# Four edge hops gather with no bounds check, and targets without out-edges read a row of zeros

## The reference, cut to what matters

```
src = randint(0, 100000, (50000,));  dst = randint(0, 100000, (50000,))
A = 0.9 * segment_softmax(scores, head_ids)          # one weight per edge and head, 4 heads
Z = broadcast(x[:, None, :], (N, 4, 64))
for _ in range(5):
    Z = segment_sum(A[:, :, None] * Z[tail_ids], head_ids) + 0.1 * x[:, None, :]
out = Z.reshape(N, 256) @ W_o
```

## Time and profile before

| | us |
|---|---|
| median of 3 runs | 12004.88 (11990.27 to 12047.62) |
| the profiled execution | 12010.07 |
| its span, first to last instruction | 12007.8 |
| hop 1, first gather to hop 2's first gather | 543.5 |
| GpSimd busy | 7991.8 (67%) |
| VectorE busy | 6262.3 (52%) |

### The profile page before, as it was taken

The page is one execution under the profiler, slowest core; times in us unless marked ns, Lnnn a source line. Parts: engine busy times, 40 slices in busy tenths (PEclk is TensorE's granted clock), DMA queues, the critical chain, the costliest instruction groups (busy, mean ns, idle before and its releaser), DMA issues. The chain is left out here.

```text
span 12007.8 us, 102357 instructions
## 1 busy us (share of the span) xinstructions
PE 5179.3 (43%) x22423; PEld 3584.6 (30%) x22423; DVE 6262.3 (52%) x12751; ACT 2459.6 (20%) x4317; POOL 7991.8 (67%) x7869
## 2 busy tenths in 40 slices
PE   1719994000000244445656678843335422222245
PEld 1403331000000144444444556622224322222234
DVE  8931115767878644465545669943336533321127
ACT  0102221022222211122323333310003200000035
POOL 1767774776767677753767666657767677777730
PEclk9959997555555555566767777755556555555578
DMA  2412222544545311167655556622229833311148
GB/s 107 165 20 58 57 58 72 167 136 151 165 149 166 104 40 42 41 215 211 168 155 167 178 185 191 194 75 59 59 54 312 246 65 65 65 47 46 46 152 251
DMA packets 1247797, 1471.21 MB, mean 123 GB/s; under 512 B 843713, under 2 KB 948738, under 8 KB 1244410
## 3 DMA queue, kind: packets, MB, share of 16 engines
q1 hardware_dynamic: 951992, 1127.40, 29.7%
q0 software_dynamic: 277328, 269.94, 10.7%
q10 hardware_dynamic: 18290, 72.03, 1.5%
HBM read 830.95 MB, written 772.36 MB: 134 GB/s over the span
## 5 line engine op out<-in xcount | busy, mean ns | idle before, releaser
L2541 POOL DMA_INDIRECT r_got<-state,comb_src x1176 | 1218.2, 1036 | 449.3 <-issue 350.1
L328 POOL DMA_INDIRECT payload_or_bias_rows<-payload,place x784 | 875.5, 1117 | 669.6 <-issue 260.4
L1330 POOL DMA_INDIRECT hop_got<-edges_b,next_col x784 | 790.7, 1009 | 271.8 <-issue 238.0
L1330 POOL DMA_INDIRECT hop_got<-edges_a,next_col x784 | 783.4, 999 | 265.5 <-issue 238.2
L1579 PE MATMUL hop_ps_into<-hop_out,span_s 128*128 128x256 f32 (+1 forms) x10 | 5.6, 660 | 2046.4 <-DVE hop_out L1471 2045.1
L1519 ACT COPY hop_got<-hop_zeros 128x1792 f32<-128x1792 f32 x224 | 377.4, 1685 | 1514.9 <-DVE hop_ps_msg L1422 1102.8
L1579 PEld LDWEIGHTS hop_ps_into<-hop_out,span_s 128*128 128x128 f32 x10 | 2.5, 311 | 2048.9 <-DVE hop_out L1471 2047.3
L1471 DVE SCALAR_TENSOR_TENSOR hop_out<-hop_out,hop_runs_now,hop_ps_msg 128x256 f32<-128x256 f32 x1176 | 565.5, 481 | 51.0
L1342 POOL DMA_INDIRECT sum<-hop_out,put_s x392 | 432.2, 1103 | 119.5 <-issue 119.5
L2678 DVE TENSOR_REDUCE r_stat<-r_sq 128x14 f32<-128x896 f32 x196 | 211.9, 1081 | 571.1 <-ACT r_sq L2848 570.8
L2549 POOL DMA_INDIRECT x<-r_yt,put_t x392 | 403.9, 1030 | 143.8 <-issue 118.9
(11 more groups left out here) (727 smaller groups left out, 16871.7 us busy)
## 6 DMA issues: line engine op xcount, KB each, us to landing
edges_a<-hop_out SPq DMA_DIRECT2D x112, 896.0 KB
edges_b<-hop_out SPq DMA_DIRECT2D x112, 896.0 KB
hop_side<-x_dst SPq DMA_DIRECT2D x280, 224.0 KB, 4.0
r_in<-state SPq DMA_DIRECT2D x112, 448.0 KB, 4.7
x_and_sums<-c_y SPq DMA_DIRECT2D x56, 896.0 KB, 5.6
bn_in<-x_and_sums SPq DMA_DIRECT2D x56, 896.0 KB, 4.9
r_own<-state SPq DMA_DIRECT2D x84, 448.0 KB, 5.3
g_rows<-r_gx SPq DMA_DIRECT2D x84, 448.0 KB, 2.9
```

Of the source, the lines that this page charges most:

```text
L328: nc.gpsimd.indirect_dma_start(out=rows[:, n, :], out_offset=None, in_=t.pay, in_offset=bass.IndirectOffsetOnAxis(t.place[:, k, n:n + 1], ...
L1330: pool.indirect_dma_start(out=got[:, u, c, :], out_offset=None, in_=table, in_offset=at, bounds_check=EP - 1, oob_is_err=False).then_inc(g ...
L2541: pool.indirect_dma_start(out=got[:, n, c - b * CT, :], out_offset=None, in_=table, in_offset=bass.IndirectOffsetOnAxis(idx[:, at + c:at + ...
```

## The change

The gathers of hops 1 to 4 lose their bounds check. An edge whose target has no out-edges now fetches row EP of the table, which is zeros, so each gather always moves 128 rows of 1 KB. The tile of zeros, its clearing by VectorE, the 4 first copies and the 224 later copies by ScalarE and the semaphores `zeroed` go. GpSimd waits instead for `added`, the moment at which VectorE has read the buffer, and in the first round of the ring it waits for nothing.

```
-        if heads and table is not None:
-            zeros = sb("zeros", [P, CT, G])
...
                 if heads:
-                    pool.wait_ge(zeroed[u], i + 1)
+                    wait(pool, added, n + 1 - RING)
...
                 for c in range(CT):
                     at = bass.IndirectOffsetOnAxis(idx[:, n * CT + c:n * CT + c + 1], 0)
-                    if heads:
-
-                        pool.indirect_dma_start(out=got[:, u, c, :], out_offset=None, in_=table, in_offset=at,
-                                                bounds_check=EP - 1, oob_is_err=False).then_inc(gathered[u], 16)
-                    else:
-                        pool.indirect_dma_start(out=got[:, u, c, :], out_offset=None, in_=table, in_offset=at
-                                                ).then_inc(gathered[u], 16)
+                    pool.indirect_dma_start(out=got[:, u, c, :], out_offset=None, in_=table, in_offset=at
+                                            ).then_inc(gathered[u], 16)
...
-            if heads and table is not None:
-                nc.vector.memset(zeros[:], 0.0)
             nc.vector.memset(acc[:, 1, CT - 1, 0:M], 0.0).then_inc(blank, 1)
...
-            if heads and table is not None:
-                act.wait_ge(blank, 1)
-                for u in range(RING):
-                    nc.scalar.copy(got[:, u], zeros[:]).then_inc(zeroed[u], 1)
...
-                    if heads and table is not None:
-                        act.wait_ge(added, order(i, u) + 1)
-                        nc.scalar.copy(got[:, u], zeros[:]).then_inc(zeroed[u], 1)
```

More of the change, by code:

```diff
@@ L1285, in edge_pass @@
         linked, blank, added = sem("linked"), sem("blank"), sem("added")
-        runs_ready, side_scaled, zeroed = sems("runs_ready"), sems("side_scaled"), sems("zeroed")
+        runs_ready, side_scaled = sems("runs_ready"), sems("side_scaled")
         rt_done, rt_read, gt_done, gt_read, lin_done = sem("rt_done"), sem("rt_read"), sem("gt_done"), sem("gt_read"), sem("lin_done")
```

## The result

The changed kernel takes 12098.5 us (median of 4, 12089.69 to 12114.59) against 12009.9 us before (median of 4, 11990.27 to 12047.62). The ratio is 1.0076, with a 95% interval of 1.0059 to 1.0093. It is slower by 89 us, where +63 was forecast. The profiled execution took 12114.59 us, with a span of 12112.8.

The account below looks back on a forecast made before the run. GpSimd paced all hops, 9.13 us a chunk in hops 1 to 3; DMA engines would bind those at 9.74: +102 us, hop 4 -21, starts -18, +63 on 12010, median 5 less: 12070 us. Range 11895 to 12230.

Parts of the forecast that it names:

- The check: Gathers of hops 1 to 4: dropping the bounds check saves GpSimd 0.054 us each, 84.7 us in all where GpSimd paces.
- The start of a hop: At each of four hop starts the first gather goes 4.4 us earlier, without zero-tile clearing and first copy: 17.6 us.
- The place: In HBM, repeated reads queue at places about 256 bytes wide, so 77 reads of the zero row take 0.9 us a gather.
- The sum of the two kinds of work: Hops 1 to 3: SyncE's transfers and the gathers add on the DMA engines, 3.44 + 6.3 = 9.74 us a chunk.
- this case: The forecast's own case: 8.9 to 10.4 us a chunk in hops 1 to 3, 11930 to 12180 us, chance 0.45.
- the term for the gathers: DMA engines' time for a chunk's seven gathers, each 0.9 us: 6.3 us.
- SyncE's share: DMA engines' time for SyncE's transfers in a chunk of hops 1 to 3: 3.44 us.
- The wait: Hops 1 to 3: VectorE would wait longer for the gathers, and GpSimd for `added`, with some 575 us a hop.
- GpSimd as pacer everywhere: Rival: zero-row reads and stores share the DMA engines without loss, GpSimd paces at 8.75 us a chunk; 11903 us, chance 0.27.
- The single place: Rival: the 1 KB zero row is one place or two; over 15,000 us at one, 13130 at two; chance 0.14.
- the check that costs nothing: Rival: the gathers' 0.054 us is the row size's, not the check's; 11987 us hidden, 12091 if DMA-bound; chance 0.06.
- the higher price: Rival: the forecast's mechanism in hops 1 to 3 at 10.44 to 12.2 us a chunk; 12185 to 12480 us, chance 0.08.

Follow-up runs that it names:

- e3_check_kept: e1_spread with a bounds check kept on the hops' gathers, its limit raised to the last zero row so nothing is skipped: 11983.04 us, ratio 0.9979.
- e8_probe: Changed kernel plus series of 8 single, waited-for gathers behind hop 4, reading the same place, different rows or two rows: 12331.34 us, one run.
- e2_two_rows: As e1_spread, but with two zero rows only, partitions 0 to 63 reading row EP and the others EP + 1: 11894.07 us, ratio 0.9902.
- e4_all_zero_row: Changed kernel with all 128 indices of every gather in hops 1 to 4 set to row EP, target sums left out: 12737.52 us, one run.
- e5_small_store: Changed kernel storing a seventh in hops 1 to 3, all hops gathering from the table hop 0 wrote: 11911.57 us, one run.
- e1_spread: Changed kernel with reads of zero row EP spread to row EP + p of each partition p: 11896.3 us, ratio 0.9912 to the kernel before.
- e6_side_ring4: Changed kernel with SyncE's loads in hops 1 to 3 given four buffers instead of two and issued two chunks earlier: 12105.6 us, ratio 1.0068.

## Why the prediction was right

**The check** was priced at 0.054 us a gather from other layers' rows, and measured 0.052 (e3_check_kept) and 0.053 (the changed kernel).

**The start of a hop** was put at 4.4 us. In e3_check_kept the first gather goes 4.0 us earlier, and a hop is 4.7 us shorter.

**The place.** The prediction read a width of 256 bytes, or nearly, out of a broadcast's 221 GB/s. What the forecast needs of it holds: a row of 1 KB read again and again costs no more than a piece of 256 bytes does (e8_probe), and neighbouring rows of 256 bytes don't share a place (the later gather of e2_two_rows). That a row is read as pieces side by side remains an inference. The 0.9 us for 77 reads hold too: e4_all_zero_row gives 0.0113 us a read in the time of a hop, 0.87 us for 77.

**The sum of the two kinds of work** was the step on which the sign hung, since at 8.75 us a chunk the change would have gained 102 us. The changed kernel's 9.97 us and e4_all_zero_row, whose 51 further reads a gather lengthen the hop by 0.0113 us each, bear out that time is added and not hidden. e5_small_store shows that it takes the full store for this. e1_spread, 111 us under the kernel before by medians, shows the gain of about 102 us that the repetition took away. But the terms are not constants: by its own queue shares a gather holds the engines 0.61 us in e5_small_store and 0.93 in the changed kernel, so adding fixed shares was right in its result and is open in its mechanism. The prediction had given this case 0.45.

**What was off is a size.** With e1_spread's hop as 56 x 8.75 + 28.2 us, the changed kernel's chunk is (586.3 - 28.2)/56 = 9.97 us (VectorE's turns give 9.98), against 9.74 forecast: 0.23 us, which over 168 chunks is 39 us. By its queue shares the chunk has 6.54 us of gathers, 0.93 each where 0.90 was taken, 2.88 us of SyncE's transfers where 3.44 was taken, and 0.55 us in which the engines are not counted as busy. So the term for the gathers was 0.24 us a chunk too small. SyncE's share was 0.56 us smaller than in the kernel before, for a reason that no run shows, and the idle time, which I had left out, is 0.55 us. That the two cancel is luck. Hop 4 gave back more than forecast, 34 us where 21 had been put (its start counts in hop 3's interval), though hop 4 ranges from 1036 to 1048 us in the seven other kernels whose check is gone, so some of this is scatter. The forecast of 12070 us is 28 us under the measured median.

**The wait.** The profile was to show VectorE waiting longer for the gathers. In hop 2 it waited 22.3 us for them and 105.8 us for ScalarE, which waited for SyncE's late loads. That full DMA engines would delay the loads first was not foreseen; it changes nothing in the sum, since e6_side_ring4 moves the wait and not the time. The other signs came as said: 0.946 us a gather, no register moves beside the hops' gathers, the first gather within 1 us of SyncE's first load, 131 KB a gather and a DMA share of 0.88.

**The rivals.** GpSimd as pacer everywhere (11903 us) did not come about, but it is what e1_spread and e2_two_rows measure, 11896 and 11894 us. The single place, the check that costs nothing and the higher price are excluded, in this order, by e8_probe, by e3_check_kept, and by the 9.97 us a chunk.

On the Trainium skill: the rule of "DMA: Bandwidth & Descriptors", section "Anatomy of one DMA — SWDGE (gpsimd) path", about 2.0 us plus the bytes at 436 GB/s, gives as estimates 2.08 us for 32.8 KB and 2.3 us for 131 KB. In the traces different rows land after 2.4 or 2.5 us (256 bytes) and 3.0 us (1 KB, e1_spread), and the same row costs 1.2 us on top in the probe. The rule has no term for the addresses, and here they decide.

## What to carry to other kernels

A padding index that many gathers share is a cost of its own: give the padding several rows. Here two did as well as one for each partition (hops of 518.3 and 518.2 us), and the rows were there already. Before bytes are added behind a paced engine, add up what all queues take of the DMA engines in one turn of the loop, with the price of the worst addresses, and compare the sum, not each part, with the pace. Take such a sum as a warning and not as a time, because the shares grow in company (0.61 against 0.91 us a gather here). Where a trace names a late load on a full set of DMA engines, look at the share first: here moving the load moved the wait and gained 15 us of 1760.

## What the hardware showed

- Many reads of one row of HBM queue up, at 0.0113 us a read in the hops (e4_all_zero_row; 22.7 GB/s if counted for 256 bytes) and 0.0075 to 0.0092 us in the probe. A row of 512, 1024 or 2048 bytes read 128 times takes only 0.04, 0.15 or 0.3 us longer than one of 256.
- The DMA engines' busy share of the same gather depends on what runs beside it: 0.61 us with a seventh of the store, 0.91 us with all of it.
- A second row takes most of it away: two rows of 1 KB, 64 readers each, cost 3.26 us a turn against 3.91 for one and 2.96 for 128.
- The bounds check of an indirect DMA costs GpSimd 0.052 us when it skips nothing (e3_check_kept), and 0.053 us when it skips 77 of 128 rows (the kernel before).
